# A recurrence and a mixture of experts on one TensorE: the last product of each tile part one step later, the copy of the down products one place on, the bank seedings three steps further

## The chip, the cores and the metric

One core of a Trainium2 chip runs the whole kernel; the other cores are idle. The metric is the device time of one execution in microseconds (us), shown as the median of three runs, and beside it the time of one profiled execution from which all rows below are taken.

## What is computed

A tanh recurrence of 1024 steps runs over two sequences. Each of its outputs goes through a router that picks two of eight experts, through those experts, and is added to the input. Cut to what matters:

```python
# x: (2, 1024, 256); Wx, Wh: (256, 256); wg, wu: (8, 1024, 256); wd: (8, 256, 1024)
xW = einsum('ntd,dh->nth', x, Wx) + b
def step(prev_h, xw_t):
    next_h = tanh(xw_t + prev_h @ Wh)
    return next_h, next_h
hs = scan(step, cond_1024, xW over t)
logits = hs @ gate_w.T
top_v, top_i = top_k(logits, 2)
combine = softmax(top_v) spread over the 8 experts
for e in range(8):
    hidden = silu(hs @ wg[e].T) * (hs @ wu[e].T)
    acc = acc + combine[e][:, None] * (hidden @ wd[e].T)
return x + acc
```

## The kernel before, in words

All numbers are held as a high and a low half in fp16, and a product of two such numbers is made of three products of halves.

**The steps.** The code of every engine is one long list of steps `n` = 32 to 1055, one for each step of the recurrence. TensorE opens a step with `state_products(n)`: four products with `wh_hi` that finish the pre-activation of step `n` (and start that of step `n + 3`); it waits for the state of the step before (`s_next`). Four products with `wh_lo` (`low_weights`) follow. ScalarE then makes the full state (`L843`, a tanh into a PSUM bank) and, three steps early, the high half (`L835`); VectorE subtracts to get the low half (`L1175`), and that releases TensorE's next step. All three engines work off their instructions in the order of the code, so what a step adds behind these stands between one turn of this ring and the next. 64 steps make a block (`blk`, with `tt` the step in the block).

**The tiles.** From step 240 on, TensorE has expert work in each step, behind the eight state products. 24 steps make a tile (`p`, with `o` the place in the tile, 0 to 23): 34 of them in the steps, the first 30 of them 128 rows wide, the others 64, and a few more behind the last step. A tile is two halves of 12 steps, and a half has six parts of two steps: gate, up, and down products (`gate_up`, `L597`; `down`, `L619`), where the down products of a half follow half a tile later. `tile(p, o, n)` cuts a part of 24 units (12 wide products) into two shares, one for each step, 12 units each, or 14 and 10 where one of the two steps is `heavy` with other work. What is left of 14 units in a step is filled with idle products (`keep_warm`, `L628`).

**What the other engines do for a tile.** ScalarE applies silu at places 2 and 8 of a half, when the gate part is done (`s_g`). VectorE multiplies with the up products at places 4 and 10. When the second half of the previous tile has all its down products (`s_d`), ScalarE copies them out of PSUM (`copy_yT`, `L815`, at place `YT_AT`); TensorE turns them with two transposes (`turn_y`, `L576`, at places `Y_TURN_AT` = 13 and 14), the first of which waits for the copy (`s_yt`); ScalarE weighs them at place 15, and GpSimd adds them to the output by an indirect DMA (`L1373`) at place 16. Another indirect DMA (`L1350`) writes rows of the recurrence to the experts' lists, at places 0, 6 or 12.

**The seedings.** The pre-activations lie in three PSUM banks. In three steps of each block, VectorE writes the bias into one bank each for the next block (`L1181`), right behind its low half; ScalarE's `L843` of the following step then waits for that too (`s_clr`), beside its wait for TensorE.

Of the kernel before, what the change touches and what calls it, by code (L numbers as in the profile page):

```python
# [31 lines left out]

TURN_ROWS_AT = (3, 4)
TANH_AT, RANK_AT, X_HI_AT = 12, 14, 16
LEAD = 3
TICKS = 19
FIRST = 32
START, PERIOD, HALF_T = 208 + FIRST, 24, 12
R = 64
WIDE, WIDE_FIRST = 30, 6  # L40
FRONT_AT = range(FIRST + 25, FIRST + 121, 12)
UNITS, FIRST_UNITS, FIRST_STEPS = 14, 24, 6
SILU_AT, HI_AT = (2, 8), (5, 11)
MUL_AT, LO_AT = (4, 10), (6, 0)
YT_AT, WEIGH_AT, X_OUT_AT = 12, (15, 18), (21, 22)
Y_TURN_AT, X_TURN_AT = (13, 14), (19, 20)
SLICE_AT, TAKE_AT, SHIFT_AT, PASS_AT = (7, 8, 9, 11), 19, (13, 14), 15
ADD_AT, SCATTER_AT = (16, 22), (0, 6, 12)
# [4 lines left out]
def build(nc, xT, x, h0T, wx, wh, bias, gateT, w_all, tok0, out):  # L53
# [7 lines left out]
    NBLK = -(-N // STEPS)  # L61
# [12 lines left out]
    NPAIR = (N - START) // PERIOD  # L74
# [29 lines left out]
    def first(blk):  # L104
        return 0 if blk else FIRST

    def x_hi_at(blk):
# [3 lines left out]
        at = [tt for tt in range(X_HI_AT, STEPS) if tt not in copies and not busy_act(blk * STEPS + tt)][0]  # L111
        assert at + 2 + 36 <= STEPS - LEAD
        return at
# [23 lines left out]
    with ExitStack() as ctx:  # L137
# [132 lines left out]
        s_zh = sem("hi_products_done")  # L270
        s_clr = sem("xw_seeded")
# [56 lines left out]
        def made_before(n):  # L328

            return n - FIRST + 1 + min(n, N - LEAD) - FIRST  # L330

        def seeds(n):

            blk, t = divmod(n, STEPS)
            return blk < NBLK - 1 and t - first(blk) < 3

        def two(first, second):

# [9 lines left out]
        def wide(p):  # L348
            return fixed(p) and p < WIDE

        def expert(p, half):
            return (p + WIDE_FIRST) % E if wide(p) else 2 * (p % (E // 2)) + half
# [93 lines left out]
        def _(pe):  # L446
# [185 lines left out]
            def heavy(n):  # L632
                return pair_of(n)[1] in Y_TURN_AT + X_TURN_AT or (n >= STEPS and n % STEPS in (0,) + TURN_ROWS_AT)

            def tile(p, o, n):

                half, w = divmod(o, HALF_T)
                part, sub = divmod(w, 2)
                fewer = HALF_T + 2 * (heavy(n ^ 1) - heavy(n))
                n0, n1 = (2 * HALF_T - fewer, 2 * HALF_T) if sub else (0, fewer)  # L640
                pq, hq = (p, 0) if half else (p - 1, 1)
                t = pq if part in (2, 5) else p
                if t < 0:
                    return 0
                if wide(t):
                    m0, m1 = n0 // 2, n1 // 2
                else:
                    m0, m1 = n0, n1
                if part in (2, 5):
                    down(pq, hq, expert(pq, hq), part // 3, m0, m1)  # L650
                else:
                    gate_up(p, half, expert(p, half), int(part in (1, 4)), part // 3, m0, m1)
                return n1 - n0

            def free_cols(o):

# [58 lines left out]
            def finish_pair(p, e):  # L715
                for g in range(2):
                    down(p, 1, e, g, 0, ALL)
# [21 lines left out]
            g = NBLK - 1  # L739
            pe.wait_ge(s_next, made_before(N))  # L740
            logits(g % 2, g)
            finish_pair(NPAIR - 1, expert(NPAIR - 1, 1))
            for part in range(2):
                turn_rows(g % 2, g, part)
# [28 lines left out]
        def _(act):  # L773
# [63 lines left out]
            def step(blk, i, tt):  # L837
                n = blk * STEPS + tt
                p, o = pair_of(n)
                if blk < NBLK - 1 and tt - first(blk) in (1, 2, 3):  # L840
                    act.wait_ge(s_clr, 3 * blk + tt - first(blk) + 3)
                act.wait_ge(s_pre, n - FIRST + 1)
                act.activation(h32_at(n), preact(n), ACT.Tanh, scale=1 / SCALE).then_inc(s_h32, 1)  # L843
                if n + LEAD < N:
                    hi_of(n + LEAD, s_next)
                if p >= 0:
                    half, w = divmod(o, HALF_T)
                    if p == 0 and o == SILU_AT[0]:
                        act.wait_ge(s_cl, 2 * NCH)
                    if w in SILU_AT:  # L850
                        silu(p, half, SILU_AT.index(w))
                    if w in HI_AT:
                        hidden_hi(p, half, HI_AT.index(w))
                    if p >= 1 and o == YT_AT:
                        copy_yT(p - 1)
                    if p >= 1 and o in WEIGH_AT and (o == WEIGH_AT[0] or not wide(p - 1)):
                        weigh(p - 1, WEIGH_AT.index(o))
                if p >= -1 and o in X_OUT_AT:
                    x_out(p + 1, X_OUT_AT.index(o))
                if blk:  # L860
                    if tt in rows_at(blk):
                        copy_rows(blk - 1, rows_at(blk).index(tt))
                    if tt == TANH_AT:
                        tanh_weight(blk - 1)
                if blk < NBLK - 1 and tt == x_hi_at(blk):
                    act.wait_ge(s_x, 16 * (blk + 2))
                    act.wait_ge(s_xw, blk + 1)
                    act.copy(x_hi, xt).then_inc(s_xhi, 1)
                if split_of(blk, tt) is not None:
                    split(split_of(blk, tt))  # L870
# [59 lines left out]
        def _(v):  # L930
# [239 lines left out]
            def step(blk, i, tt):  # L1170
                n = blk * STEPS + tt
                p, o = pair_of(n)
                last = blk == NBLK - 1
                v.wait_ge(s_h32, n - FIRST + 1)
                v.tensor_tensor(lo[:, i, :, B * tt:B * tt + B],  # L1175
                                h32_at(n).rearrange("p (c b) -> p c b", c=2),
                                hi[:, i, :, B * tt:B * tt + B], ALU.subtract).then_inc(s_next, 1)
                if seeds(n):

                    v.wait_ge(s_zh, LEAD + 3 * blk + tt - first(blk) + 1)  # L1180
                    v.tensor_copy(xw[(n + 2) % 3][:, (1 - i) * P:(1 - i) * P + SEEDS], seed_cols).then_inc(s_clr, 1)  # L1181
                if not last and tt == x_hi_at(blk) + 1:
                    v.wait_ge(s_xhi, blk + 2)
                    v.tensor_tensor(x_lo, xt, x_hi, ALU.subtract).then_inc(s_xlo, 1)
                if tt and split_of(blk, tt - 1) is not None:
                    split(split_of(blk, tt - 1))
                if tt == 0 and blk and split_of(blk - 1, STEPS - 1) is not None:
                    split(split_of(blk - 1, STEPS - 1))
                if p >= -1:
                    tile(p, o)  # L1190
                if blk:
                    tick = tt if tt < RANK_AT else tt - late(blk)
                    if tt < RANK_AT or tick >= RANK_AT:
                        route(1 - i, blk - 1, tick)
                    if n == count_step(blk):
                        count(blk - 1)
                if n >= N - 4:
                    make_slice(NPAIR + 1, n - (N - 4))
# [247 lines left out]
```

## Time and profile before

| what | value |
|---|---|
| median of 3 runs | 847.75 us (846.58 to 849.95) |
| profiled execution, its own time | 847.57 us |
| its span, first to last instruction | 845.5 us |
| TensorE busy, matmuls | 741.6 us (88%) |
| ScalarE busy | 479.4 us (57%) |
| VectorE busy | 441.4 us (52%) |
| share of TensorE in the chain that ended last | 78% |

The span is what lies between the first and the last instruction that the profile recorded; 2.07 us of the execution's time lie around it. Busy shares are means over all stages. The chain that ended last goes back from the last instruction, at each step to what released it.

### The profile page before, as it was taken

The page shows a single profiled execution, that of the slowest core. Times are in us where ns is not written, and L with a number is a line of the kernel's source. Part 1 is how long each engine was busy: PE and PEld are TensorE (multiplying, and loading weights), DVE is VectorE, ACT ScalarE, POOL GpSimd, SP SyncE. Part 2 cuts the span into 40 slices and gives each one's busy share as a digit, 9 for nine tenths or more (in the row PEclk, how much of TensorE's full clock was granted, in tenths as well). Part 3 has the DMA queues.
Part 4 walks back from the last instruction along what each step waited for, and adds up shares of the span by engine and source line. Part 5 has one row for each costly group of instructions (what it writes and reads, how often), then busy time and mean ns, then how long its engine had stood idle before and what let it go on. Part 6 is the DMA issues. An engine that isn't in the chain of part 4 may idle for free.

```text
span 845.5 us, 41906 instructions
## 1 busy us (share of the span) xinstructions
PE 741.6 (88%) x17106; PEld 645.1 (76%) x17106; DVE 441.4 (52%) x2572; ACT 479.4 (57%) x2839; POOL 112.0 (13%) x104
## 2 busy tenths in 40 slices
PE   6555555699999999999999999999999999998894
PEld 4443444588888888888888888888888888887784
DVE  4776767454454545454544445454545444455542
ACT  4776777555555555555655556555555555554442
POOL 1000000001111101101020111111021101123222
PEclk7555555599999999999999999999999999999997
DMA  4676766501111111111120111111111111111111
GB/s 131 194 198 183 205 186 184 183 10 38 19 35 22 35 22 24 34 20 31 22 41 16 29 23 34 29 26 25 19 39 22 34 16 29 24 17 39 29 29 23
DMA packets 35149, 49.01 MB, mean 58 GB/s; under 512 B 5232, under 2 KB 21616, under 8 KB 34928
## 3 DMA queue, kind: packets, MB, share of 16 engines
q1 hardware_dynamic: 27200, 36.53, 15.7%
q0 software_dynamic: 7488, 9.57, 7.2%
q8 instruction: 134, 2.20, 1.1%
q14 instruction: 55, 0.45, 0.2%
q10 hardware_dynamic: 272, 0.26, 0.1%
HBM read 35.57 MB, written 12.88 MB: 57 GB/s over the span
## 4 chain that ended last, share of the span: by engine, by line
PE 78%; DVE 6%; ACT 6%; DMA 4%; issue 4%; another core or an unknown queue 0%; POOLq 0%; ACTq 0%; SPq 0%; DVEq 0%
PE bank L474 35%; PE bank L597 24%; PE bank L619 12%; DVE state L1175 4%; ACT bank L843 4%; DMA arena<-w_all 3%; PE bank L628 3%; PE bank L456 1%; PE bank L576 1%; DMA out<-y_sb,place_now 1%; PE bank L568 1%; ACT w_hi L829 1%; DVE arena L1103 0%; DMA b_sb<-bias_in 0%
## 5 line engine op out<-in xcount | busy, mean ns | idle before, releaser
L1175 DVE TENSOR_TENSOR state<-bank,state 128x4 f16<-128x4 f32 x1024 | 166.1, 162 | 353.7 <-ACT bank L843 339.3
L474 PE MATMUL bank<-state,wh_hi 128*128 128x4 f16 (+1 forms) x4204 | 264.8, 168 | 83.1 <-DVE state L1175 74.0
L843 ACT ACTIVATE bank<-bank 128x4 f32<-128x4 f32 x1024 | 161.9, 158 | 306.1 <-PE bank L474 300.4
L474 PEld LDWEIGHTS bank<-state,wh_hi 128*128 128x128 f16 x4204 | 176.5, 98 | 172.4 <-DVE state L1175 115.3
L474 PE MATMUL bank<-state,wh_lo 128*128 128x2 f16 x4096 | 245.4, 163 | 0.0
L474 PEld LDWEIGHTS bank<-state,wh_lo 128*128 128x128 f16 x4096 | 177.5, 97 | 0.0
L835 ACT ACTIVATE state<-bank 128x4 f16<-128x4 f32 x1024 | 175.1, 171 | 2.8 <-PE bank L474 2.7
L597 PE MATMUL bank<-x_T,w_hi 128*128 128x128 f16 (+1 forms) x1856 | 154.8, 206 | 4.6 <-issue 2.6
L619 PE MATMUL bank<-arena,w_hi 128*128 128x128 f16 (+1 forms) x1600 | 140.1, 208 | 0.3 <-DVE arena L1110 0.2
L597 PE MATMUL bank<-x_T,w_lo 128*128 128x128 f16 (+1 forms) x928 | 138.1, 206 | 0.0
L597 PE MATMUL bank<-arena,w_hi 128*128 128x128 f16 (+1 forms) x1344 | 129.0, 211 | 1.7 <-issue 1.3
L619 PE MATMUL bank<-arena,w_lo 128*128 128x128 f16 (+1 forms) x800 | 125.7, 208 | 0.0
L597 PEld LDWEIGHTS bank<-x_T,w_hi 128*128 128x128 f16 x1856 | 110.2, 97 | 6.3 <-issue 3.2
L597 PE MATMUL bank<-arena,w_lo 128*128 128x128 f16 (+1 forms) x672 | 113.4, 211 | 0.6 <-issue 0.4
L456 PE MATMUL bank<-early 128*128 128x42 f16 (+1 forms) x612 | 109.6, 193 | 1.3 <-DVE early L1219 1.3
L628 PE MATMUL bank<-wh_hi 128*128 128x64 f16 (+3 forms) x511 | 103.0, 210 | 0.0
L619 PEld LDWEIGHTS bank<-arena,w_hi 128*128 128x128 f16 x1600 | 95.8, 97 | 0.7 <-DVE arena L1110 0.4
L1373 POOL DMA_INDIRECT out<-y_sb,place_wide x30 | 47.5, 1583 | 361.7 <-ACT y_sb L823 361.7
L597 PEld LDWEIGHTS bank<-arena,w_hi 128*128 128x128 f16 x1344 | 86.3, 97 | 2.8 <-issue 2.1
L597 PEld LDWEIGHTS bank<-x_T,w_lo 128*128 128x128 f16 x928 | 86.3, 97 | 0.1
L829 ACT ACTIVATE w_hi<-arena 128x256 f16<-128x256 f32 x192 | 80.6, 420 | 4.4 <-DMA arena<-w_all 4.4
L1150 DVE SCALAR_TENSOR_TENSOR w_lo<-arena,w_hi 128x256 f16<-128x256 f32 x192 | 79.6, 414 | 0.0
(141 smaller groups left out, 971.4 us busy)
## 6 DMA issues: line engine op xcount, KB each, us to landing
arena<-w_all SPq DMA_DIRECT2D x96, 256.0 KB
xrow<-expert_rows SPq DMA_DIRECT2D x82, 66.0 KB
early<-xT SPq DMA_DIRECT2D x17, 128.0 KB
expert_rows<-pad SPq DMA_DIRECT2D x8, 132.0 KB, 3.2
expert_rows<-rows,slot POOLq DMA_INDIRECT x34
out<-y_sb,place_wide POOLq DMA_INDIRECT x30
out<-y_sb,place_now POOLq DMA_INDIRECT x20, 3.2
arena<-wh_in ACTq DMA_DIRECT2D x1, 256.0 KB, 4.2
```

Source lines behind the costliest of these rows:

```text
L456: return pe.matmul(dst, w[:, k, m * P:(m + 1) * P], mv, start=False, stop=False, skip_group_check=True)
L474: return pe.matmul(out, w[:, k, m * P:(m + 1) * P], moving, start=False, stop=False, skip_group_check=True)
L568: mm = pe.transpose(p_x[:, c * P:(c + 1) * P], xrow16[:, c * P:(c + 1) * P], ident16[:])
L597: mm = pe.matmul(dst[:, at + c * cols:at + (c + 1) * cols], w[:, e, col:col + P], xs[:, xpart, 0:P] if wide(p) else xs[:, xpart, half * R: ...
L619: mm = pe.matmul(p_yT[:, a:a + cols], w[:, e, col:col + P], part[half][:, g * QW + c * cols:g * QW + (c + 1) * cols], start=(opens and n = ...
L628: pe.matmul(dst[:, 0:min(n, 4) * R], wh_hi[:, 0, 0:P], wh_hi_cols[:, 0:min(n, 4) * R], start=False, stop=True, skip_group_check=True)
L829: act.activation(w_hi_cols[:, cols], half_stage(n), ACT.Copy, scale=SCALE).then_inc(s_ch, 1)
L835: act.activation(hi[:, i, :, c:c + B], src, ACT.Tanh, scale=1 / SCALE).then_inc(made, 1)
L843: act.activation(h32_at(n), preact(n), ACT.Tanh, scale=1 / SCALE).then_inc(s_h32, 1)
L1150: v.scalar_tensor_tensor(out=w_lo_cols[:, cols], in0=half_stage(n), scalar=SCALE, in1=w_hi_cols[:, cols], op0=ALU.mult, op1=ALU.subtract). ...
L1175: v.tensor_tensor(lo[:, i, :, B * tt:B * tt + B], h32_at(n).rearrange("p (c b) -> p c b", c=2), hi[:, i, :, B * tt:B * tt + B], ALU.subtra ...
L1373: pool.indirect_dma_start(out, bass.IndirectOffsetOnAxis(ap=place_wide[:, 0:1], axis=0), y_sb[:], None, compute_op=ALU.add).then_inc(s_sca ...
```

## The change

Three constants and the functions that use them.

- `tile` leaves the last two units of each part (`LATER`; one product of a wide tile, two of a narrow one) for the first step of the next part, where they come ahead of that part's own products. Each step keeps its number of units. Behind the last step, one such rest is made up after the logits.
- `YT_AT` goes from 12 to 13: ScalarE copies the down products one step later. `Y_TURN_AT` stays at (13, 14).
- `seed_at` puts the three seedings of a block, from block 1 on, into steps 3 to 5 of it where they were in steps 0 to 2.

```diff
+SEED_AT = 3
...
+LATER = 2
...
-YT_AT, WEIGH_AT, X_OUT_AT = 12, (15, 18), (21, 22)
+YT_AT, WEIGH_AT, X_OUT_AT = 13, (15, 18), (21, 22)
...
+        def seed_at(blk):
+            return SEED_AT if blk else FIRST
+
         def seeds(n):
 
             blk, t = divmod(n, STEPS)
-            return blk < NBLK - 1 and t - first(blk) < 3
+            return blk < NBLK - 1 and 0 <= t - seed_at(blk) < 3
...
+            def units_of(p, half, part, n0, n1):
+
                 pq, hq = (p, 0) if half else (p - 1, 1)
                 t = pq if part in (2, 5) else p
                 if t < 0:
                     return 0
...
+                m0, m1 = (n0 // 2, n1 // 2) if wide(t) else (n0, n1)
                 if part in (2, 5):
                     down(pq, hq, expert(pq, hq), part // 3, m0, m1)
                 else:
                     gate_up(p, half, expert(p, half), int(part in (1, 4)), part // 3, m0, m1)
                 return n1 - n0
+
+            def tile(p, o, n):
+
+                half, w = divmod(o, HALF_T)
+                part, sub = divmod(w, 2)
+                fewer = HALF_T + 2 * (heavy(n ^ 1) - heavy(n))
+                if sub:
+                    return units_of(p, half, part, 2 * HALF_T - fewer - LATER, 2 * HALF_T - LATER)
+                if part:
+                    done = units_of(p, half, part - 1, 2 * HALF_T - LATER, 2 * HALF_T)
+                else:
+                    done = units_of(p - 1 + half, 1 - half, 5, 2 * HALF_T - LATER, 2 * HALF_T)
+                return done + units_of(p, half, part, 0, fewer - LATER)
...
             pe.wait_ge(s_next, made_before(N))
             logits(g % 2, g)
+            units_of(NPAIR - 1, 1, 5, 2 * HALF_T - LATER, 2 * HALF_T)
             finish_pair(NPAIR - 1, expert(NPAIR - 1, 1))
...
-                if blk < NBLK - 1 and tt - first(blk) in (1, 2, 3):
-                    act.wait_ge(s_clr, 3 * blk + tt - first(blk) + 3)
+                if blk < NBLK - 1 and tt - seed_at(blk) in (1, 2, 3):
+                    act.wait_ge(s_clr, 3 * blk + tt - seed_at(blk) + 3)
...
-                    v.wait_ge(s_zh, LEAD + 3 * blk + tt - first(blk) + 1)
+                    v.wait_ge(s_zh, LEAD + 3 * blk + tt - seed_at(blk) + 1)
```

How it moves instructions is shown at two places, both in tile 2. First TensorE at place 12, where the down products of tile 1 end and the second gate half of tile 2 begins (in the changed kernel's line numbers `L479` is `L474`, `L602` is `L597`, `L624` is `L619`, `L461` is `L456`, `L581` is `L576`). Before:

```order
L474 MATMUL bank0<-state,wh_hi 128x2x2 [waits h_lo_and_early_h_hi]
L474 MATMUL bank0<-state,wh_hi 128x2x2 x3
L474 MATMUL bank2<-state,wh_lo 128x2 x4
L597 MATMUL bank3<-x_T,w_hi 128x128 [waits silu_done]
L597 MATMUL bank3<-x_T,w_hi 128x128
```

Now:

```order
L479 MATMUL bank0<-state,wh_hi 128x2x2 [waits h_lo_and_early_h_hi]
L479 MATMUL bank0<-state,wh_hi 128x2x2 x3
L479 MATMUL bank2<-state,wh_lo 128x2 x4
L624 MATMUL bank6<-arena,w_lo 128x128
L602 MATMUL bank3<-x_T,w_hi 128x128 [waits silu_done]
```

One down product (into bank 6) has moved from the end of the step before to here, ahead of the wait of the new part.

Then TensorE at place 13, from the state products to the first transpose and the state products of place 14. Before:

```order
L474 MATMUL bank1<-state,wh_hi 128x2x2 [waits h_lo_and_early_h_hi]
L474 MATMUL bank1<-state,wh_hi 128x2x2 x3
L474 MATMUL bank0<-state,wh_lo 128x2 x4
L597 MATMUL bank3<-x_T,w_hi 128x128
L597 MATMUL bank3<-x_T,w_lo 128x128
L597 MATMUL bank3<-x_T,w_hi 128x128 x2
L597 MATMUL bank3<-x_T,w_lo 128x128
L456 MATMUL bank0<-early 128x21x2
L576 MATMUL bank5<-ident32,arena 128x128 [waits pair_T,yT_copied]
L474 MATMUL bank2<-state,wh_hi 128x2x2 [waits h_lo_and_early_h_hi]
```

Now:

```order
L479 MATMUL bank1<-state,wh_hi 128x2x2 [waits h_lo_and_early_h_hi]
L479 MATMUL bank1<-state,wh_hi 128x2x2 x3
L479 MATMUL bank0<-state,wh_lo 128x2 x4
L602 MATMUL bank3<-x_T,w_hi 128x128 x2
L602 MATMUL bank3<-x_T,w_lo 128x128
L602 MATMUL bank3<-x_T,w_hi 128x128 x2
L461 MATMUL bank0<-early 128x21x2
L581 MATMUL bank5<-ident32,arena 128x128 [waits pair_T,yT_copied]
L479 MATMUL bank2<-state,wh_hi 128x2x2 [waits h_lo_and_early_h_hi]
```

TensorE's list has the transpose at the same place in the step as before, behind five products and one for the next block.

The same two steps on ScalarE, place 12 from the first `L843` on and place 13 from the second. Before:

```order
L843 ACTIVATE bank1<-bank0 128x4 [waits preact]
L835 ACTIVATE state<-bank0 128x2x2
L815 COPY arena<-bank6 128x256 [waits y_turned,down_done]
L843 ACTIVATE bank2<-bank1 128x4 [waits preact]
L835 ACTIVATE state<-bank1 128x2x2
```

Now (`L855` is `L843`, `L847` is `L835`, `L827` is `L815`):

```order
L855 ACTIVATE bank1<-bank0 128x4 [waits preact]
L847 ACTIVATE state<-bank0 128x2x2
L855 ACTIVATE bank2<-bank1 128x4 [waits preact]
L847 ACTIVATE state<-bank1 128x2x2
L827 COPY arena<-bank6 128x256 [waits y_turned,down_done]
```

The copy that the transpose waits for now stands behind the two tanh of place 13, the step of the transpose itself.

## Rows read from the trace of the kernel before

**Rows 1.** Timeline, places 12 to 14 of tile 1: start us, length us, engine, line, operation, tiles.
```profile
210.54 0.16 ACT L843 ACTIVATE bank<-bank 128x4 f32<-128x4 f32 x1 [0.17 <-PE bank L474]
...
210.66 0.38 ACT L815 COPY arena<-bank 128x256 f32<-128x256 f32 x1
...
211.25 0.16 ACT L843 ACTIVATE bank<-bank 128x4 f32<-128x4 f32 x1 [0.20 <-PE bank L474]
...
211.44 0.16 DVE L1175 TENSOR_TENSOR state<-bank,state 128x4 f16<-128x4 f32 x1 [0.21 <-ACT bank L843]
...
211.45 0.14 PEld L576 LDWEIGHTS bank<-ident,arena 128*128 128x128 f32 x1
...
211.65 0.17 PEld L474 LDWEIGHTS bank<-state,wh_hi 128*128 128x128 f16 x4
...
211.87 0.27 PE L597 MATMUL bank<-x_T,w_hi 128*128 128x128 f16 x2
...
212.07 0.39 ACT L801 ACTIVATE arena<-bank 128x256 f32<-128x256 f32 x1
```

**Rows 2.** Line L576 in the steps (0 to 766 us): lengths in ns.
```profile
L576 PE MATMUL bank<-ident,arena x66: 278/307/309, 194.1 to 757.7; 128*128 128x128 f32 x66
```

**Rows 3.** Timeline behind the last loop: the last copy and the last two transposes.
```profile
834.44 0.37 ACT L815 COPY arena<-bank 128x256 f32<-128x256 f32 x1
834.95 0.20 PEld L576 LDWEIGHTS bank<-ident,arena 128*128 128x128 f32 x2 [0.67 <-ACT x_T L793]
```

**Rows 4.** Timeline of TensorE behind the last step: two transposes in a row.
```profile
769.81 0.42 PE L576 MATMUL bank<-ident,arena 128*128 128x128 f32 x2
```

**Rows 5.** Timeline, the first two seedings' steps of block 9.
```profile
411.50 0.16 ACT L843 ACTIVATE bank<-bank 128x4 f32<-128x4 f32 x1 [0.17 <-PE bank L474]
...
411.77 0.24 DVE L1181 COPY bank<-early 128x88 f32<-128x88 f32 x1
...
412.26 0.16 ACT L843 ACTIVATE bank<-bank 128x4 f32<-128x4 f32 x1 [0.52 <-PE bank L474]
```

**Rows 6.** Timeline, three steps that meet an indirect DMA of GpSimd.
```profile
353.13 0.16 ACT L843 ACTIVATE bank<-bank 128x4 f32<-128x4 f32 x1
...
353.31 1.61 POOL L1373 DMA_INDIRECT out<-y_sb,place_wide  x1 [6.29 <-ACT y_sb L823]
...
354.78 0.16 ACT L843 ACTIVATE bank<-bank 128x4 f32<-128x4 f32 x1 [0.33 <-PE bank L474]
...
317.59 0.16 ACT L843 ACTIVATE bank<-bank 128x4 f32<-128x4 f32 x1
...
317.77 1.56 POOL L1373 DMA_INDIRECT out<-y_sb,place_wide  x1 [15.44 <-ACT y_sb L823]
...
319.14 0.16 ACT L843 ACTIVATE bank<-bank 128x4 f32<-128x4 f32 x1 [1.31 <-PE bank L474]
...
244.82 0.16 ACT L843 ACTIVATE bank<-bank 128x4 f32<-128x4 f32 x1 [0.17 <-PE bank L474]
...
244.93 1.00 POOL L1350 DMA_INDIRECT expert_rows<-rows,slot  x1 [12.60 <-ACT arena L809]
...
246.26 0.16 ACT L843 ACTIVATE bank<-bank 128x4 f32<-128x4 f32 x1 [0.93 <-PE bank L474]
```

**Rows 7.** Line L843 from 193 to 691 us: instructions, first and last start.
```profile
L843 ACT ACTIVATE bank<-bank x684: 158/158/167, 193.1 to 690.9; 128x4 f32<-128x4 f32 x171
```

**Rows 8.** Chain that ended last: six gate products at the tiles' start.
```profile
166.62 0.66 PE bank L597 x6
...
168.08 0.36 PE bank L597 x6
```

**Rows 9.** Windows: length, busy us (instructions) of PE, PEld, DVE, ACT, POOL, granted clock.
```profile
165.00:168.00 3.00, 3.00 (x44) 2.71 (x41) 0.32 (x2) 0.48 (x4) 0.00 (x0) 0.53 0.15 46
...
316.00:322.00 6.00, 5.22 (x121) 4.59 (x121) 2.99 (x19) 2.88 (x18) 1.56 (x1) 1.00 0.24 27
```

**Rows 10.** Timeline: TensorE's next state products in the last of these windows.
```profile
319.55 0.25 PE L474 MATMUL bank<-state,wh_hi 128*128 128x4 f16 x4 [0.78 <-DVE state L1175]
```

More of the change, by code:

```diff
@@ L633, in heavy @@
                 return pair_of(n)[1] in Y_TURN_AT + X_TURN_AT or (n >= STEPS and n % STEPS in (0,) + TURN_ROWS_AT)
[L635 to L640, printed above, removed]
+            def units_of(p, half, part, n0, n1):
                 pq, hq = (p, 0) if half else (p - 1, 1)
@@ L644, in tile @@
                     return 0
[L645 to L648, printed above, removed]
+                m0, m1 = (n0 // 2, n1 // 2) if wide(t) else (n0, n1)
                 if part in (2, 5):
```

## The prediction

> **What bounds the kernel now.** I read the page first: TensorE is busy 88% of the span and holds most of the chain that ended last. A busy TensorE need not be its limit, so I went to the timeline of two plain steps in the tile stage [rows 1]. The reader is to see a ring. ScalarE's tanh L843 starts at 210.54 and again at 211.25, 0.71 us later. VectorE's L1175 ends at 211.44 + 0.16 = 211.60, and TensorE loads the next state products at 211.65. TensorE's other work of a step fits inside the ring, and so does what ScalarE and VectorE do for the tiles. A step therefore costs about 0.70 us as long as nothing is put between the links. Next I counted steps over the wide tiles [rows 7]: 684 tanh from 193.1 to 690.9, so 683 steps in 497.8 us, 0.729 us each. That is 0.029 us over 0.70, or 19.8 us in this stretch: what there is to lose or win beside the ring itself. Then I looked for where it sits. Steps that meet an indirect DMA of GpSimd are long [rows 6]; the steps with a seeding are 412.26 - 411.50 = 0.76 us, 0.06 over [rows 5].
>
> **The change, part by part.**
>
> **The copy one place on.** This part decides. In [rows 1] the copy L815 runs at place 12, 210.66 to 211.04, and the transpose L576 that waits for it loads at 211.45, in the step after. It never waits. Now the copy belongs to place 13, the transpose's own step, and ScalarE takes it behind both tanh. At place 12 it starts 210.66 - 210.54 = 0.12 us after L843. Behind the L843 of place 13, at 211.25, it would run 211.37 to 211.75. The transpose stands ahead of the next state products in TensorE's list, so the ring waits for it.
>
> When would the next state products load? Before: 211.65. Now three links follow the copy's end.
> - Release of TensorE. The nearest row of the same kind is the end of the program, where the transposes waited for this very copy [rows 3]: end 834.44 + 0.37 = 834.81, load 834.95, so 0.14. The nearest row inside the steps is VectorE's release of the state products, 211.60 to 211.65, so 0.05 [rows 1]. The transpose would load at 211.80 to 211.89, against 211.45 before.
> - Passage of the transpose. Two in a row take 0.42 us [rows 4] where one takes 0.307 at the median [rows 2], so the next instruction is 0.11 behind. From below, the two loads in [rows 3] take 0.20 where one takes 0.14 [rows 1]: 0.06 behind. From above, 211.45 to 211.65, 0.20 behind [rows 1], though there the ring itself set the time.
> - With 0.11 the state products load at 211.91 to 212.00, so 0.26 to 0.35 us late. I take the middle, 0.31. The outer ends are 0.05 + 0.06, late by 0.21, and 0.14 + 0.20, late by 0.44.
>
> Nothing else in that step covers it: VectorE's low half is ready at 211.60 whatever the copy does. Nor does the next step win it back, since the ring of place 14 starts when those products start. The second transpose (place 14) finds its input ready; weighing and the addition follow later, as far behind the ring as before. [rows 2] count 66 transposes in the steps, two per tile, so 33 tiles pay: 33 x 0.31 = 10.2 us, with ends 33 x 0.21 = 6.9 and 33 x 0.44 = 14.5.
>
> One question is whether TensorE could pull the next weight loads past the waiting transpose. [rows 3] show its load unit idle for 0.67 us, and only the transposes' own loads behind it. The Trainium skill (TensorE: Matmul & The Clock Gate, "Architectural detail: the array is 16× 32×32, not 1× 128×128") says that TensorE's queue is a partial reorder window that pulls weight loads ahead of matmuls in flight, while ScalarE and VectorE keep strict order. By the first half the state loads could be done during the wait and the sum would be nearer its lower end, 6.9 us; by the second, ScalarE cannot take the copy ahead of its tanh, and the wait stands. The row speaks for no more than the second, and I keep 10.2.
>
> **The last product one step later.** No step gets more products, so TensorE's work per step stays. What is late is the end of a part. The gate part's last product now is the first product behind the state products; in [rows 1] that place is 211.87, and two products there end by 212.14. Silu L801 starts at 212.07, so it may start up to 0.07 late and end at 212.53 for 212.46. Its engine's next tanh comes at 211.25 + 2 x 0.70 = 212.65, so 0.12 us of cover is left, and the cost is nothing. If the cover were gone, each 0.01 us at four places of 33 tiles would be 1.3 us. I see no gain either: no plain step waits for a part's end. Behind the last step one product or two change places with the logits: nothing.
>
> **The seedings.** The 0.06 us of [rows 5] belongs to the extra wait and moves with it. L1181 takes 0.24 us of VectorE and now stands beside other router work. Fully exposed once in each of 15 blocks it would cost 15 x 0.24 = 3.6; if the 0.06 vanished in all three steps it would win 15 x 3 x 0.06 = 2.7. I take nothing: it still follows the low half directly, so only what is queued behind it moves, and that has the rest of the step.
>
> **Sum.** The profiled execution's 847.57 + 10.2 = 857.8 us. It lies 0.18 under the median of the runs, so beside the median I forecast 858.0.
>
> **The rivals.**
>
> *The collisions go.* A step that meets GpSimd's DMA loses 354.78 - 353.13 - 1.40 = 0.25 us in the common case. At 317.59 to 319.14, with a seeding in the step, it loses 0.85; at 244.82 to 246.26, with the copy in the step, 0.74 [rows 6]. Both companions move away. By the 24-step and 64-step rhythm there are three of the first and four of the second in the wide tiles: 3 x 0.60 + 4 x 0.49 = 3.8 us back, so 857.8 - 3.8 = 854.0. Against it: in both, ScalarE waits for TensorE, whose step is fuller there (logits, a 14-unit share), and that stays. Chance 0.10.
>
> *Faster: TensorE's backlog under GpSimd's DMAs dissolves.* Of the 19.8 us in [rows 7], the seedings hold 10 x 3 x 0.06 = 1.8. If all the rest were a backlog of products that a part's end makes, and the moved product freed it, 18.0 us would come back: 857.8 - 18.0 = 839.8. It decides when more than 10.2 of those 18.0 go, over half. Against it: the number of products per step is the same. Chance 0.04.
>
> *The wait is hidden.* If something else holds the next state products as long as the transpose, the time stays at 847.6. Nothing in [rows 1] is that late. Chance 0.06.
>
> *The clock falls.* The first six gate products took 0.66 us at a granted clock of 0.53, mostly the lower level of 1.2 GHz, and 0.36 soon after [rows 8, 9]. If TensorE's new idle time let the clock drop for one step per tile, 33 x 0.30 = 9.9 us would come on top: 867.7. Against it: TensorE sat idle 0.78 us before 319.55 [rows 10], longer than any wait here, and the granted clock around it is 1.00, full 2.4 GHz [rows 9]. The Trainium skill (TensorE: Matmul & The Clock Gate, "What's actually happening") has it that an idle array falls back to half its clock; here the trace shows no fall after such an idle time. Chance 0.04.
>
> **How the numbers follow.** The wait in the transpose's step as costed: 0.74. Collisions 0.10, hidden 0.06, faster 0.04, clock 0.04; other 0.02. Only the hidden wait, the faster case and small parts of others lie below 852.0. The likeliest case alone spans 854.5 to 862.1 by its ends. Taking in the collisions case at 854.0 and a mix of it with the lower end, the range is 853 to 862.5. Half a per cent, 4.2 us, is about what a measurement of this kernel can tell from no change. Slower by more: 0.87; within: 0.08; faster: 0.05.
>
> **What would show it.** Right: the transpose of place 13 loads 0.05 to 0.14 us after the copy's end, with a wait for the copy named in 33 rows, and the step from place 13 to 14 is 0.96 to 1.05 us. The steps that meet GpSimd's DMAs keep their lengths, and seeding steps stay 0.76. Wrong: a step of 0.70 at place 13; or long GpSimd steps gone by more than the transposes cost; or plain steps shorter than 0.70.

## The result, and the profile after

The changed kernel took 859.1 us (median of 4 runs, 858.11 to 861.16) where the kernel before took 848.54 (median of 4, 846.58 to 849.95). The ratio is 1.0126, with a 95% interval of 1.0103 to 1.0149: slower by 10.6 us. The forecast was 858.0, in 853 to 862.5. The profiled execution is the slowest of the four, 861.16 us, and its span 859.1 is 13.6 over the 845.5 of before.

The page of the changed kernel: span, busy times, and in 40 slices the busy share of TensorE and its granted clock.

```profile
span 859.1 us, 41908 instructions
...
PE 749.0 (87%) x17107; PEld 650.3 (76%) x17107; DVE 441.2 (51%) x2572; ACT 485.0 (56%) x2839; POOL 112.1 (13%) x104
...
PEclk7555555599999999999999999999999999998997
```

No engine has more work than before: TensorE runs 17107 matmuls for 17106, and one idle product is the whole difference. Its busy time is 7.4 us longer all the same, and 87% of the longer span for 88%. The mean says little here. The ring does, and the counterpart of [rows 1] is the timeline of places 12 to 14 of the same tile, now with the line numbers of the changed kernel. (In the code's count it is tile 2, `p` = 2; [rows 1] calls it tile 1.)

```profile
212.68 0.16 ACT L855 ACTIVATE bank<-bank 128x4 f32<-128x4 f32 x1 [0.17 <-PE bank L479]
...
213.09 0.25 PE L479 MATMUL bank<-state,wh_hi 128*128 128x4 f16 x4
...
213.38 0.16 ACT L855 ACTIVATE bank<-bank 128x4 f32<-128x4 f32 x1 [0.46 <-PE bank L479]
...
213.50 0.38 ACT L827 COPY arena<-bank 128x256 f32<-128x256 f32 x1
213.57 0.16 DVE L1187 TENSOR_TENSOR state<-bank,state 128x4 f16<-128x4 f32 x1 [0.21 <-ACT bank L855]
...
213.93 0.14 PEld L581 LDWEIGHTS bank<-ident,arena 128*128 128x128 f32 x1 [0.31 <-ACT arena L827]
213.93 0.33 PE L581 MATMUL bank<-ident,arena 128*128 128x128 f32 x1 [0.17 <-ACT arena L827]
213.94 0.31 PEld L479 LDWEIGHTS bank<-state,wh_hi 128*128 128x128 f16 x4
214.10 0.24 PE L479 MATMUL bank<-state,wh_hi 128*128 128x4 f16 x4
...
214.38 0.16 ACT L855 ACTIVATE bank<-bank 128x4 f32<-128x4 f32 x1 [0.50 <-PE bank L479]
```

Read the tanh L855 first: 212.68, 213.38, 214.38. The step from place 12 to 13 takes 0.70 us, the next one 1.00. Then follow what ended last in the long one. VectorE's low half is done at 213.57 + 0.16 = 213.73. The copy runs 213.50 to 213.88, and 0.05 behind it the transpose loads, with the copy named in its bracket. The state products run 0.17 behind the transpose, at 214.10, where 213.09 + 0.70 = 213.79 would have been their turn.

That this is one of 33, and that before there was none, is seen in the view of one line and those who wait for it. First the copy in the changed kernel, up to 780 us:

```profile
L827 ACT COPY arena<-bank x33: 380/380/381, 195.4 to 769.2; 128x256 f32<-128x256 f32 x33
...
who waited for it (us, times):
  PEld bank L581: 13.6, 33
```

The same view of the kernel before has nobody who waited for L815. Taken over all starts of L855, the 33 steps that begin at place 13 of these tiles lie 10.4 us over 0.70 each in sum, and lay 0.2 over before: 10.2 us more. 27 of them take 1.00 us, two 1.10 that were 0.80 before, and four 1.06: these four now also meet a seeding, which accounts for 0.24 of the 10.2. The wait itself is 9.9 us, 0.30 for each tile.

Then the steps that meet a DMA of GpSimd, the counterparts of the last two in [rows 6], and one more at place 6:

```profile
322.23 0.16 ACT L855 ACTIVATE bank<-bank 128x4 f32<-128x4 f32 x1
322.41 1.56 POOL L1385 DMA_INDIRECT out<-y_sb,place_wide  x1 [15.71 <-ACT y_sb L835]
...
323.72 0.16 ACT L855 ACTIVATE bank<-bank 128x4 f32<-128x4 f32 x1 [1.25 <-PE bank L479]
...
247.61 0.16 ACT L855 ACTIVATE bank<-bank 128x4 f32<-128x4 f32 x1 [0.17 <-PE bank L479]
247.72 1.00 POOL L1362 DMA_INDIRECT expert_rows<-rows,slot  x1 [12.69 <-ACT arena L821]
...
249.01 0.16 ACT L855 ACTIVATE bank<-bank 128x4 f32<-128x4 f32 x1 [1.16 <-PE bank L479]
...
207.80 0.16 ACT L855 ACTIVATE bank<-bank 128x4 f32<-128x4 f32 x1 [0.17 <-PE bank L479]
207.90 0.97 POOL L1362 DMA_INDIRECT expert_rows<-rows,slot  x1 [3.37 <-ACT arena L821]
...
209.18 0.16 ACT L855 ACTIVATE bank<-bank 128x4 f32<-128x4 f32 x1 [1.14 <-PE bank L479]
```

The first takes 1.49 us for 1.55 in [rows 6], with the seeding gone from it; the second 1.40 for 1.44, with the copy gone. Both companions moved away and the long steps stayed. The third is new, 1.38 us. Its step before the change was short:

```profile
206.17 0.16 ACT L843 ACTIVATE bank<-bank 128x4 f32<-128x4 f32 x1 [0.17 <-PE bank L474]
206.27 0.97 POOL L1350 DMA_INDIRECT expert_rows<-rows,slot  x1 [3.40 <-ACT arena L809]
...
206.88 0.16 ACT L843 ACTIVATE bank<-bank 128x4 f32<-128x4 f32 x1 [0.47 <-PE bank L474]
...
207.74 0.16 ACT L843 ACTIVATE bank<-bank 128x4 f32<-128x4 f32 x1 [0.63 <-PE bank L474]
```

There the DMA costs 0.01 us in its own step and 0.16 in the next; now it costs 0.68 in its own and nothing in the next. That is 0.51 us net, and four of the seven such steps of the wide tiles have turned long, so 2.0 us in this execution. 10.2 at place 13 and 2.0 here are 12.2 of the 13.6 us. Another 1.2 lies in two steps at the head of the first tile, 1.47 and 1.48 us where they were 0.86 each: in this execution the granted clock was still at its lower level there (the lines stand with the clock, below). 0.9 lies behind the last tanh, and all other steps together are 0.7 shorter.

The seedings, one block with [rows 5] as counterpart:

```profile
420.20 0.16 ACT L855 ACTIVATE bank<-bank 128x4 f32<-128x4 f32 x1
...
420.48 0.24 DVE L1193 COPY bank<-early 128x88 f32<-128x88 f32 x1
420.96 0.16 ACT L855 ACTIVATE bank<-bank 128x4 f32<-128x4 f32 x1 [0.52 <-PE bank L479]
```

420.96 - 420.20 = 0.76 us, as before.

### The profile page after: what moved, and what is told of

Its sections match the earlier page's. It is cut to its first block, busy times and chain, and to the rows that moved or that the text cites. A ratio compares the mean times of both kernels' runs of the same rounds, so it can differ in the third digit from the quotient of the medians.

```text
span 859.1 us, 41908 instructions
## 1 busy us (share of the span) xinstructions
PE 749.0 (87%) x17107; PEld 650.3 (76%) x17107; DVE 441.2 (51%) x2572; ACT 485.0 (56%) x2839; POOL 112.1 (13%) x104
## 4 chain that ended last, share of the span: by engine, by line
PE 76%; ACT 7%; DVE 6%; DMA 5%; issue 4%; another core or an unknown queue 0%; POOLq 0%; ACTq 0%; SPq 0%; DVEq 0%
PE bank L479 33%; PE bank L602 24%; PE bank L624 12%; DMA arena<-w_all 5%; ACT bank L855 4%; DVE state L1187 4%; PE bank L633 3%; PE bank L581 2%; PE bank L461 1%; PE bank L573 1%; ACT arena L827 1%; ACT state L847 1%; ACT w_hi L841 1%; DVE arena L1115 1%; DVE w_lo L1162 1%
## 5 line engine op out<-in xcount | busy, mean ns | idle before, releaser
L855 ACT ACTIVATE bank<-bank 128x4 f32<-128x4 f32 x1024 | 161.9, 158 | 312.1 <-PE bank L479 292.7
L479 PE MATMUL bank<-state,wh_hi 128*128 128x4 f16 (+1 forms) x4204 | 265.1, 168 | 81.4 <-DVE state L1187 73.3
L479 PEld LDWEIGHTS bank<-state,wh_hi 128*128 128x128 f16 x4204 | 181.8, 99 | 167.8 <-DVE state L1187 111.9
L479 PE MATMUL bank<-state,wh_lo 128*128 128x2 f16 x4096 | 245.4, 163 | 0.0
L479 PEld LDWEIGHTS bank<-state,wh_lo 128*128 128x128 f16 x4096 | 177.7, 97 | 0.0
L847 ACT ACTIVATE state<-bank 128x4 f16<-128x4 f32 x1024 | 175.0, 171 | 2.8 <-PE bank L479 2.7
L602 PE MATMUL bank<-x_T,w_hi 128*128 128x128 f16 (+1 forms) x1856 | 157.1, 207 | 4.5 <-DVE arena L1115 2.0
L624 PE MATMUL bank<-arena,w_hi 128*128 128x128 f16 (+1 forms) x1600 | 145.0, 209 | 0.0
L602 PE MATMUL bank<-x_T,w_lo 128*128 128x128 f16 (+1 forms) x928 | 142.0, 206 | 0.0
L624 PE MATMUL bank<-arena,w_lo 128*128 128x128 f16 (+1 forms) x800 | 134.5, 209 | 0.0
L602 PE MATMUL bank<-arena,w_hi 128*128 128x128 f16 (+1 forms) x1344 | 131.7, 211 | 1.8 <-issue 1.5
L602 PEld LDWEIGHTS bank<-x_T,w_hi 128*128 128x128 f16 x1856 | 115.9, 97 | 6.1 <-issue 3.1
L602 PE MATMUL bank<-arena,w_lo 128*128 128x128 f16 (+1 forms) x672 | 117.6, 211 | 0.6 <-issue 0.5
L461 PE MATMUL bank<-early 128*128 128x42 f16 (+1 forms) x612 | 109.7, 194 | 1.3 <-DVE early L1231 1.3
L624 PEld LDWEIGHTS bank<-arena,w_hi 128*128 128x128 f16 x1600 | 105.8, 98 | 0.5
L602 PEld LDWEIGHTS bank<-arena,w_hi 128*128 128x128 f16 x1344 | 92.7, 97 | 3.1 <-issue 2.5
L602 PEld LDWEIGHTS bank<-x_T,w_lo 128*128 128x128 f16 x928 | 86.1, 97 | 0.1
```

The source lines that it names most:

```text
L461: return pe.matmul(dst, w[:, k, m * P:(m + 1) * P], mv, start=False, stop=False, skip_group_check=True)
L479: return pe.matmul(out, w[:, k, m * P:(m + 1) * P], moving, start=False, stop=False, skip_group_check=True)
L602: mm = pe.matmul(dst[:, at + c * cols:at + (c + 1) * cols], w[:, e, col:col + P], xs[:, xpart, 0:P] if wide(p) else xs[:, xpart, half * R: ...
L624: mm = pe.matmul(p_yT[:, a:a + cols], w[:, e, col:col + P], part[half][:, g * QW + c * cols:g * QW + (c + 1) * cols], start=(opens and n = ...
L847: act.activation(hi[:, i, :, c:c + B], src, ACT.Tanh, scale=1 / SCALE).then_inc(made, 1)
```

## The experiments

Theory A: the copy in the transpose's own step makes TensorE wait, at 0.30 us for each of 33 tiles, and the two other edits cost next to nothing. Its rivals blame these other edits or GpSimd's DMAs. Twelve kernels were run, in three groups of four. Each ratio is to the kernel before on the same chip, whose median was 852.31, 848.14 and 850.44 us in the three groups.

**The copy undone, and each part alone.** The changed kernel with the copy back:

```diff
-YT_AT, WEIGH_AT, X_OUT_AT = 13, (15, 18), (21, 22)
+YT_AT, WEIGH_AT, X_OUT_AT = 12, (15, 18), (21, 22)
```

> The changed kernel with the copy of the down products put back to place 12, the late product and the moved seedings kept. Theory A (the transpose of place 13 waits for a copy in its own step, 0.30 us in each of 33 tiles): the step from place 13 to 14 is 0.70 us again and 33 x 0.30 = 9.9 us go, so about 849 us for the changed kernel's 859, level with the kernel before (ratio 0.998 to 1.005). Rival B (the late product or the seedings carry the loss, the copy only shows it): the step at place 13 gets shorter, but the time stays above 855. Rival C (part of the loss sits in steps that meet GpSimd's row scatter at place 6, which became 0.5 us longer in 5 of 7 tiles in the changed kernel): 849 to 852, and these long steps are still there.

Measured: 851.56 us, 0.9998 (0.9981 to 1.0015). The whole loss is gone. Two of the seven steps at place 6 are still long, as rival C has it, without showing in the time. (The expectation counts five of them in the changed kernel's profile; among the seven of the wide tiles it is four.)

The kernel before with the copy alone moved, the same line the other way:

> The kernel before with the copy alone put to place 13. Theory A: 848.5 + 9.9 = 858.4 us, ratio about 1.0117, every step from place 13 to 14 of a wide tile about 1.00 us. Rival B: under 852, since the late product is not there. Rival C: 858, and the steps at place 6 that meet the row scatter keep the 0.18 us over 0.70 of the kernel before, in place of 0.68.

Measured: 863.11 us, 1.0122 (1.0095 to 1.0150). This one constant makes as much loss as the whole change, within the intervals. None of the seven steps at place 6 is long. The copy's view shows the same wait as in the changed kernel:

```profile
L815 ACT COPY arena<-bank x33: 379/379/380, 194.1 to 771.5; 128x256 f32<-128x256 f32 x33
...
  PEld bank L576: 13.5, 33
```

The kernel before with the late product alone (`LATER = 2` and the new `tile`), and with the seedings alone (`seed_at`):

> The kernel before with the late product alone (copy at place 12, seedings at steps 0 to 2). Theory A: the same time within 0.5%, 846 to 852 us. If the late product moves the collision at place 6 (rival C), 5 of 7 such steps are 0.5 us longer, 2.5 us in all, and the ratio is about 1.002 to 1.003. Rival B: above 855.

Measured: 852.49 us, 1.0000 (0.9982 to 1.0017). Two of the seven steps at place 6 are long.

> The kernel before with the seedings alone moved to steps 3 to 5 of a block. Theory A: the same time within 0.3%; three steps of 0.76 us in each block at the new places, and the steps at place 16 that lost 0.85 us beside a seeding and the logits still lose 0.7 to 0.85, since the logits stay. If the seeding made that loss: 3 x 0.6 = 1.8 us less. If the seedings make the collision at place 6 worse, 2.5 us more.

Measured: 852.33 us, 0.9992 (0.9975 to 1.0008). The long steps at the blocks' starts stay, 0.81 to 0.84 us over 0.70. None at place 6 is long, but two other steps that meet a DMA of GpSimd are now, one at place 0 (1.45 us) and one at place 16 (1.48).

**The wait and not the place.** The changed kernel with the copy still at place 13, but everything behind it one place later:

```diff
-YT_AT, WEIGH_AT, X_OUT_AT = 13, (15, 18), (21, 22)
-Y_TURN_AT, X_TURN_AT = (13, 14), (19, 20)
+YT_AT, WEIGH_AT, X_OUT_AT = 13, (16, 18), (21, 22)
+Y_TURN_AT, X_TURN_AT = (14, 15), (19, 20)
```

> The changed kernel with the two transposes at places 14 and 15 and the weighing at 16, copy still at 13. Theory A (the transpose waits for a copy of its own step): the step from place 13 to 14 is 0.70 us again, the 33 x 0.30 = 9.9 us come back, and the time is level with the kernel before, ratio 0.998 to 1.003. Rival: the cost belongs to a copy at place 13 as such (ScalarE is late for its next tanh), wherever the transposes stand; then the step from 13 to 14 stays 1.00 us and the ratio 1.011 to 1.013.

Measured: 847.81 us, 1.0005 (0.9985 to 1.0024). The timeline of place 13 and the start of 14:

```profile
194.02 0.16 ACT L855 ACTIVATE bank<-bank 128x4 f32<-128x4 f32 x1 [0.46 <-PE bank L479]
...
194.14 0.38 ACT L827 COPY arena<-bank 128x256 f32<-128x256 f32 x1
194.43 0.16 PEld L479 LDWEIGHTS bank<-state,wh_hi 128*128 128x128 f16 x4
...
194.72 0.16 ACT L855 ACTIVATE bank<-bank 128x4 f32<-128x4 f32 x1 [0.20 <-PE bank L479]
...
194.98 0.14 PEld L581 LDWEIGHTS bank<-ident,arena 128*128 128x128 f32 x1
```

The copy stands where it stands in the changed kernel, 0.12 behind its tanh. The state products load at 194.43, before the copy ends at 194.52, and the step is 0.70 us. So the rival that a copy at place 13 costs by itself falls: only the transpose behind it costs. The steps that meet GpSimd's DMAs moved as well (seven long ones in the wide tiles, at other places, for eleven in the changed kernel), so some 2 us of what came back may be theirs; what decides is the step.

This run also answers for an effect of `YT_AT` that neither the change as told nor the prediction has. `busy_act` keeps the router's work on ScalarE off the places in use, `YT_AT` among them. With 13 for 12, it moves in blocks 5, 8, 11 and 14: the four copies of rows from steps 5, 8, 11 and 16 to 8, 11, 16 and 17, and one more piece of work from 17 to 19, with the products of TensorE that follow them one and two steps later. In this run the copies stand at 7, 11, 16 and 17 and the rest as in the changed kernel (four further blocks have the 19 as well), and the time is level with the kernel before. So this move costs nothing that can be measured.

**The dose.** The kernel before, with the copy at 13 in two halves, each transpose waiting for its own:

```diff
-                    pe.wait_ge(s_yt, p + 1)
+                pe.wait_ge(s_yt, 2 * p + 1 + m)
...
-                act.copy(yT, p_yT[:, 0:2 * P]).then_inc(s_yt, 1)
+                for m in range(2):
+                    act.copy(yT[:, m * P:(m + 1) * P], p_yT[:, m * P:(m + 1) * P]).then_inc(s_yt, 1)
```

> The kernel before with the copy at place 13 in two copies of 128 columns, and each transpose waiting for its own half alone. ScalarE's 256 columns take 0.38 us and its 4 columns 0.16, so 128 should take about 0.27, and the first transpose is released 0.11 us sooner than behind the whole copy. Theory A: the step from 13 to 14 is 0.30 - 0.11 = 0.19 us over, 33 x 0.19 = 6.3 us, ratio 1.006 to 1.009. Rival (the delay does not come from the length of the copy, but from the wait itself or from ScalarE's queue): 0.30 us or more over as with one copy, ratio 1.011 or more.

Measured: 854.02 us, 1.0076 (1.0048 to 1.0104). And with the halves in the other order (`for m in (1, 0)`) and the first transpose waiting for both:

> As the run with two half copies at place 13, but the second half first, and the first transpose waits for both. Theory A: two copies of about 0.27 us stand where one of 0.38 did, 0.16 us longer, so the step from 13 to 14 is 0.46 us over, 33 x 0.46 = 15 us, ratio 1.016 to 1.019. Rival (length of the copy does not matter): 0.30 us over and ratio 1.011 to 1.013.

Measured: 860.69 us, 1.0153 (1.0119 to 1.0186). With a half to wait for, the line of the copies, and then the timeline at place 13:

```profile
L816 ACT COPY arena<-bank x68: 267/273/299, 192.3 to 774.4; 128x128 f32<-128x128 f32 x68
```

```profile
192.17 0.16 ACT L844 ACTIVATE bank<-bank 128x4 f32<-128x4 f32 x1 [0.46 <-PE bank L474]
...
192.29 0.44 ACT L816 COPY arena<-bank 128x128 f32<-128x128 f32 x2
192.61 0.14 PEld L576 LDWEIGHTS bank<-ident,arena 128*128 128x128 f32 x1 [0.20 <-ACT arena L816]
...
193.06 0.16 ACT L844 ACTIVATE bank<-bank 128x4 f32<-128x4 f32 x1 [0.33 <-PE bank L474]
```

The same timeline with both to wait for:

```profile
192.46 0.16 ACT L844 ACTIVATE bank<-bank 128x4 f32<-128x4 f32 x1 [0.46 <-PE bank L474]
...
192.58 0.44 ACT L816 COPY arena<-bank 128x128 f32<-128x128 f32 x2
193.08 0.14 PEld L576 LDWEIGHTS bank<-ident,arena 128*128 128x128 f32 x1 [0.38 <-ACT arena L816]
...
193.52 0.16 ACT L844 ACTIVATE bank<-bank 128x4 f32<-128x4 f32 x1 [0.50 <-PE bank L474]
```

(`L844` is the tanh and `L816` the copy in these two kernels.) One half takes 0.273 us where the whole copy takes 0.38, so 0.11 less, and the step is 193.06 - 192.17 = 0.89: 0.19 over 0.70, as Theory A said. Both halves together take 0.44, only 0.06 more than one copy, since the second begins before the first ends; the expectation had 0.16 more, from adding two lengths, and so its sum of 15 us was too high. The step is 193.52 - 192.46 = 1.06, so 0.36 over, and 0.30 + 0.06 is just that; 33 such steps make 11.9 us, and the time is 12.6 us longer, with an interval that begins at 10.1. Three lengths of the wait (0.27, 0.38 and 0.44 us) give 0.19, 0.30 and 0.36 over: what the copy takes more, the step takes more.

**The idle products.** The kernel before with `UNITS = 0` for 14: it leaves out the idle products from the seventh tile step on, which are no part of the result.

> The kernel before without the idle products that fill a step up to 14 units (no part of the result). Of the long steps under GpSimd's DMAs: if TensorE's work in the step decides whether one is 0.2 or 0.75 us over, those with idle products in them become short, and up to 12 of them x 0.6 = 7 us come back, ratio 0.991 to 0.998. Rival: the idle products hold the clock; without them the granted clock falls below the 0.90 of before and the ratio is above 1.005. If neither, the ratio is 1.000 and the long steps stay where they are.

Measured: 851.11 us, 1.0021 (0.9999 to 1.0044), which the time alone does not settle. The long steps stay where they were, so idle products do not make them. But the mean granted clock is 0.892 over its ten executions (0.889 to 0.897), where the kernel before has 0.900 on the same chip (0.896 to 0.904). In the profile it lies at the lower level from 175 to 185 us, where the kernel before has 1.00, and falls three times more, once at this place. The windows give busy us and instructions of PE, PEld, DVE, ACT and POOL, and then the granted clock:

```profile
598.00:601.00 3.00, 2.20 (x51) 1.90 (x50) 1.12 (x7) 1.39 (x9) 1.57 (x1) 1.00 0.01 3
601.00:604.00 3.00, 3.00 (x49) 2.83 (x50) 1.70 (x12) 1.11 (x8) 0.00 (x0) 0.65 0.40 49
```

And TensorE's timeline there, where it had been idle for 0.80 us under a DMA of GpSimd:

```profile
600.99 0.25 PE L474 MATMUL bank<-state,wh_hi 128*128 128x4 f16 x4 [0.80 <-DVE state L1175]
...
601.37 0.27 PE L597 MATMUL bank<-x_T,w_hi 128*128 128x128 f16 x2
...
602.14 0.42 PE L597 MATMUL bank<-x_T,w_hi 128*128 128x128 f16 x2
```

Two gate products take 0.27 us before 602 and 0.42 after: the clock has gone to the lower level, 1.2 of 2.4 GHz. In the kernel before the window from 598 to 604 us has a granted clock of 1.00.

**The transposes later, without the rest.** The kernel before with the two lines of the run above that moves the transposes and the weighing, and the copy at 12:

> The kernel before with the transposes at places 14 and 15 and the weighing at 16, copy at 12. The transpose is now two steps behind the copy. Theory A: it never waited before either, so nothing comes back at place 13. The addition to the output moves to place 17, and other steps meet GpSimd's DMAs: one long step more or fewer is 0.6 us. Expected: within 2 us of before, ratio 0.998 to 1.002. If this beats the kernel before by over 2 us, the places of GpSimd's DMAs are worth more than thought.

Measured: 850.12 us, 0.9989 (0.9976 to 1.0003). No difference that can be measured; no version beat the kernel before. Two steps at place 0 that meet a row DMA have become long (1.43 us), and the three at the blocks' starts are short.

**The new long steps at place 6.** The copy with the seedings, the copy with the late product, and the changed kernel once more:

> The changed kernel without the late product (copy at 13 and the seedings alone). Theory: the copy's 9.9 us stay, ratio 1.011 to 1.013; the long steps at place 6 of the changed kernel's profile (four, 2.7 us) came with the late product and are gone. Rival: they come from the longer transposes' steps or the seedings and stay.

Measured: 860.02 us, 1.0107 (1.0086 to 1.0129). None of the seven is long. (The 2.7 us of the expectation are the four steps alone; with the shorter steps behind them it is 2.0.) The one of before and after above is here, where `L847` is the tanh:

```profile
206.22 0.16 ACT L847 ACTIVATE bank<-bank 128x4 f32<-128x4 f32 x1 [0.17 <-PE bank L478]
...
206.95 0.16 ACT L847 ACTIVATE bank<-bank 128x4 f32<-128x4 f32 x1 [0.50 <-PE bank L478]
```

> The changed kernel with the seedings back in the first three steps of a block (copy at 13 and the late product alone). Theory: ratio 1.011 to 1.013; of the seven steps at place 6 that meet a row DMA, some are long, as with the late product alone (two). Rival: the seedings make them long; then none is.

Measured: 861.09 us, 1.0126 (1.0100 to 1.0151). Three of the seven are long.

> The changed kernel as it is, for a second profiled execution of it. If the four long steps at place 6 are a property of its order, the same four are long again and the profiled span is again about 859 us; if they hang on a few nanoseconds, other ones of the seven are long, each worth 0.5 us.

Measured: 863.55 us, 1.0137 (1.0105 to 1.0169), profiled span 863.0. The same four are long and a fifth with them. So the late product makes these steps at place 6 long: in the six profiles with it 2 to 5 of the seven are, in the eight without it none. Which of them is long changes from run to run, so it hangs on little. It is not the only edit that does such a thing: the seedings alone and the later transposes alone made other steps long, at places 0 and 16. In time it is 2.0 us in the first profile of the changed kernel and some 2.5 in the second, and the intervals with and without it overlap.

The span here is 3.9 us over that of the first profile, and part of it is the clock, as the windows show:

```profile
248.00:251.00 3.00, 3.00 (x60) 2.88 (x61) 1.04 (x6) 1.69 (x11) 1.05 (x1) 0.78 0.03 7
251.00:254.00 3.00, 3.00 (x58) 2.92 (x56) 1.27 (x8) 1.22 (x8) 0.53 (x1) 0.65 0.38 44
```

In the first profile of the same kernel both stretches have 1.00.

## Why the prediction was right, and where it was off

**The copy.** The step named as the one that decides did decide: alone it costs 1.0122, without it the ratio is 0.9998. The wait is named in 33 rows and the step is 1.00 us, inside the 0.96 to 1.05 that was to show it. The price was put at 0.31 per tile and is 0.30, so 9.9 us for 10.2. (That the steps from place 13 on have 10.2 more than before is a coincidence: 0.24 of it are the four seedings.) That the price came out so close is in part luck, since its two parts were each off and cancelled. The release of TensorE was put between 0.05 and 0.14 and is 0.05 (213.88 to 213.93), as VectorE's release in [rows 1], and not as the program's end in [rows 3]. The passage of the transpose was put at 0.11, by two in a row in [rows 4], and is 0.17 (213.93 to 214.10): state products behind a transpose are not a second transpose.

**The weight loads.** The time would have come near the lower end of 6.9 us if loads had been pulled past the waiting transpose. They are not: TensorE's load unit is idle for 0.31 us with the copy named, and the state weights begin at 213.94, 0.01 behind the transpose's own. From there on they do run beside its matmul. With the rule of the Trainium skill (TensorE: Matmul & The Clock Gate, "Architectural detail: the array is 16× 32×32, not 1× 128×128"), that weight loads are pulled ahead of matmuls in flight, the trace agrees so far; past a transpose that waits for a semaphore none was pulled in any of the 33.

**The late product.** It was put at nothing, and by itself it is: 1.0000. The reason given, cover behind silu, looked at the wrong place, though: what it changed were steps that meet row DMAs at place 6, 2.0 us in the profiled execution. So one of the signs of being right did not hold, that the steps which meet GpSimd's DMAs keep their lengths. Nothing in the rows read gave that away, and why a DMA that met the same amount of work now costs 0.68 in its step is open; the idle products were ruled out only for the long steps that were there before.

**The seedings.** Nothing, as put: 0.76 us per step before and after, and 0.9992 alone.

**The rivals.** The collisions did not go: without the seeding a long step lost 0.79 for 0.85, without the copy 0.70 for 0.74, and the copy's wait then adds 0.30 in the next step all the same. The backlog did not dissolve, as both edits alone show. The wait was not hidden by anything. The clock did not fall tile by tile: in the window from 190 to 770 us the granted clock is 1.00, as before. It was at the lower level in two other stretches of the profiled execution, though. The windows of the changed kernel:

```profile
168.00:171.00 3.00, 3.00 (x43) 2.72 (x42) 0.33 (x2) 0.86 (x5) 0.00 (x0) 0.50 0.02 5
...
775.00:782.00 7.00, 6.42 (x130) 6.30 (x131) 4.13 (x27) 2.41 (x11) 2.43 (x2) 0.52 0.21 52
```

And of the kernel before:

```profile
168.00:171.00 3.00, 3.00 (x61) 2.84 (x58) 0.99 (x5) 1.39 (x10) 0.00 (x0) 1.00 0.02 5
```

The first is a later rise of the clock, worth the 1.2 us in two steps; in the second profile of the changed kernel the clock rises as early as in the kernel before, at 168 us, so this is no part of the change. The second, around the last tanh, is not separated from the 0.9 us there.

The reason given against the rival is also weaker than it looked. [rows 10] showed one idle time of 0.78 us without a fall, and the run without idle products shows 0.80 us with one, as does the second profile of the changed kernel behind 0.91 us. And these 0.91 us end with the waiting transpose itself. The change does add to such times: where place 12 meets a row DMA, in four tiles, TensorE is idle for 0.86 to 0.94 us up to a transpose that waits for the whole copy, while no idle time of the kernel before is over 0.80 between 190 and 766 us. Of 14 profiles, 8 have one to three short falls between 190 and 770 us, with the copy at either place, that of the changed kernel with its copy undone among them; and none has one in every tile, as the rival wanted. What settles it are all executions on record: their mean granted clock is 0.899 to 0.901 for each of the kernels in which the transpose waits, and 0.899 to 0.900 for the kernel before on the three chips. So the clock has no measurable part in the loss.

**The sum.** 847.57 + 9.9 + 2.0 = 859.5 from the parts as measured. The profiled execution took 861.16, with 1.2 more from the clock at the head of the tiles and the rest spread. The medians moved by 859.1 - 848.54 = 10.6 us where 10.2 were forecast. Most of the 1.1 us by which the forecast was low is its starting point, a median of 847.75 from three runs that four runs put at 848.54. The 2.0 us of the late product cannot be told in the medians: their interval, 1.0103 to 1.0149, is 8.7 to 12.6 us.

## What to carry to other kernels

Where engines work off their lists in order, a producer that moves into its consumer's own step can make the consumer's engine wait for as long as the producer still runs. Here the next critical work of that engine paid this in full, once per tile, whatever the busy shares said. Read it from three starts: the producer's end, the consumer's load, the next link of the ring. One more step of distance between them took the whole cost away, even with both moved.

## What the runs showed of the hardware that was not expected

- Two copies of 128 columns in a row on ScalarE take 0.44 us where one takes 0.273 and one of 256 columns 0.38: splitting a copy brings its first half 0.11 us sooner and its second only 0.06 later.
- Cutting TensorE's idle products from 103.0 to 4.3 us of its busy time lowered the mean granted clock from 0.900 to 0.892 over ten executions. At 601 us it fell behind an idle time of 0.80 us; the kernel with them has the same idle time at that place and passes it at 1.00.
- Whether a step under a DMA of GpSimd takes 0.7 or 1.4 us can turn on the order of one product, with TensorE's work in it the same, and even on the execution: the same kernel had four long steps of seven in one profile and five in the next. Why is open.
